# Routing by itself, then the shared MLP's eight tiles in one piece, in both mixtures of a macaron block

## The reference, cut to what matters

```
x = x + 0.5 * moe(layernorm(x))          # the first mixture
x = x + recurrence(layernorm(x))
x = x + 0.5 * moe(layernorm(x))          # the second mixture, same weights
x = x + 0.5 * ternary_mlp(layernorm(x)); x = x + linear_attention(layernorm(x)); x = x + 0.5 * ternary_mlp(layernorm(x))

moe(xf):                                  # 4096 x 128
    shared = gelu(xf @ Wfc_s + bfc_s) @ Wproj_s + bproj_s        # 128 -> 512 -> 128, all tokens
    logits = xf @ Wr                                             # 8 experts
    the two largest of each token, softmaxed over the two, are its gates
    routed = sum over the token's two experts of gate * (gelu(xf @ Wfc[e] + bfc[e]) @ Wproj[e] + bproj[e])
    return shared + routed
```

## Time and profile before

| what | value |
|---|---|
| median of 3 runs | 1436.36 us (1429.77 to 1442.43) |
| the profiled execution | 1437.86 us, of which the span of instructions is 1436.1 us |
| mean granted TensorE clock | 0.887 |
| busy | PE 1131.4 us (79%), DVE 930.1 us (65%), ACT 617.8 us (43%), POOL 606.4 us (42%) |
| chain that ended last | PE 31%, DVE 10% of the span |

### The profile page before, as it was taken

One profiled execution on the slowest core, in us unless ns is written; L12 is line 12 of the kernel. 1 busy time (PEld: TensorE's weight loads), 2 busy tenths in 40 slices (PEclk: granted clock), 3 DMA queues, 4 the chain that ended last, 5 costly groups with the idle time before them and its releaser, 6 DMA issues. The chain is left out here.

```text
span 1436.1 us, 17143 instructions
## 1 busy us (share of the span) xinstructions
PE 1131.4 (79%) x4972; PEld 813.5 (57%) x4972; DVE 930.1 (65%) x2723; ACT 617.8 (43%) x1114; POOL 606.4 (42%) x647
## 2 busy tenths in 40 slices
PE   5866999947689788878856667999944678888896
PEld 4645878835556555556635546888832444555453
DVE  6737787747767778777736437777752556565562
ACT  3325767734354454444522214777722122232322
POOL 5872000027676776665434743000036555542330
PEclk9878999988899999999976668999976699989997
DMA  7554567710000000000000105477721000000000
GB/s 232 192 205 178 162 216 234 244 68 24 10 13 12 10 10 12 12 8 1 1 0 15 48 34 174 152 241 251 227 69 34 15 14 18 20 15 8 8 15 16
DMA packets 48957, 115.42 MB, mean 80 GB/s; under 512 B 8160, under 2 KB 14304, under 8 KB 48864
## 3 DMA queue, kind: packets, MB, share of 16 engines
q1 hardware_dynamic: 40672, 97.53, 20.8%
q0 software_dynamic: 8192, 16.79, 3.9%
HBM read 79.16 MB, written 35.13 MB: 80 GB/s over the span
## 5 line engine op out<-in xcount | busy, mean ns | idle before, releaser
L642 DVE TENSOR_TENSOR hid_lo<-hid,hid_hi 128x512 fp32r<-128x512 f32 x248 | 170.3, 689 | 108.5 <-ACT hid L442 96.2
L491 POOL DMA_INDIRECT xs<-spare_all,slots x128 | 134.2, 1049 | 66.9 <-issue 37.4
L521 POOL DMA_INDIRECT got<-ys,y_slots x64 | 74.9, 1170 | 199.8 <-DMA ys<-spare_all 183.3
L521 POOL DMA_INDIRECT wr<-ys,y_slots x64 | 63.1, 985 | 193.5 <-DMA ys<-spare_all 177.0
L1068 DVE TENSOR_TENSOR_SCAN spare_all<-spare_all,carry 128x512 f32<-128x512 f32 x64 | 90.7, 1417 | 71.6 <-ACT spare_all L972 66.5
L442 ACT ACTIVATE hid<-bank,b_up_of 128x512 f32<-128x512 f32 x184 | 125.5, 682 | 6.0
L982 ACT ACTIVATE gate_b<-bank,head_rstd 128x128 f32<-128x128 f32 x256 | 72.9, 369 | 126.1 <-POOL head_rstd L1022 124.4
L219 PEld LDWEIGHTS bank<-ident,spare_all 128*128 128x128 f32 x568 | 76.3, 153 | 77.4 <-issue 68.7
L219 PE MATMUL bank<-ident,spare_all 128*128 128x128 f32 x568 | 94.6, 296 | 28.1 <-DVE spare_all L551 13.8
L441 ACT ACTIVATE hid_hi<-bank,b_up_of 128x512 fp32r<-128x512 f32 x138 | 95.1, 689 | 44.8 <-PE bank L364 34.6
L908 PE MATMUL bank<-spare_all,cw_sb 128*128 128x512 f32 x128 | 71.2, 640 | 33.3 <-DVE spare_all L1075 33.3
(11 more groups left out here) (263 smaller groups left out, 2894.0 us busy)
## 6 DMA issues: line engine op xcount, KB each, us to landing
wr<-wq SPq DMA_DIRECT2D x92, 512.0 KB, 4.6
spare_all<-xs SPq DMA_DIRECT2D x46, 256.0 KB, 4.8
ys<-spare_all SPq DMA_DIRECT2D x46, 256.0 KB, 4.9
wq<-wr SPq DMA_DIRECT2D x16, 512.0 KB
got<-in_w_mlp SPq DMA_DIRECT2D x9, 512.0 KB
xs<-X SPq DMA_DIRECT2D x16, 256.0 KB
xs<-spare_all,slots POOLq DMA_INDIRECT x128
out_x<-X SPq DMA_DIRECT2D x8, 256.0 KB, 2.3
```

Source lines behind the costliest of these rows:

```text
L491: g.indirect_dma_start(out=xs, out_offset=bass.IndirectOffsetOnAxis(ap=slots[:, k, n:n + 1], axis=0), in_=xn_all[:, n], in_offset=None).th ...
L521: nc.gpsimd.indirect_dma_start(out=rows_of(i, ring)[:, k, b], out_offset=None, in_=ys, in_offset=bass.IndirectOffsetOnAxis(ap=y_slots[:, k ...
L642: v.tensor_tensor(hid_lo[:, q], hid[:, n % HC], hid_hi[:, q].bitcast(F32), ALU.subtract).then_inc(s["lo_done"], 1)
```

## The change

`steps_beside` is gone. Each engine first runs its loop over the eight tiles with the routing alone, and then one loop over all 132 steps. In the first mixture the splits of the weights stay in the routing's loop. `find_blocks` moves from before step 16 to before step 4 of that second loop. The two waits about bank 5 go; in their place the first `back` waits that all eight tiles are copied.

```diff
@@ moe_pe
-                if backs_before_step(2 * i) > 0:
-                    pe.wait_ge(*s.at("finished", backs_before_step(2 * i)))
                 turn(pe, bank[5], lambda b: xn_all[:, i * TB + b]).then_inc(s["turned"], 1)
...
-                pe.wait_ge(*s.at("xT_ready", min(TILES, ((k + 2) * HC + 2) // 2 + 1)))
+                if k == 0:
+                    pe.wait_ge(*s.at("xT_ready", TILES))
...
-            for i in range(TILES + 1):
-                if i < TILES:
-                    find_logits(i)
-                for m, n in enumerate(steps_beside(i)):
-                    step(n)
-                    if m == 0 and i < TILES:
-                        find_places(i)
+            for i in range(TILES):
+                find_logits(i)
+                find_places(i)
                 if i + 1 < TILES:
                     turn_for_route(i + 1)
+            for n in range(STEPS + TAIL):
+                step(n)
@@ moe_act
-            for i in range(TILES + 1):
-                if first and i < TILES:
+            for i in range(TILES):
+                if first:
                     split_weights(i + 1)
-                for n in steps_beside(i):
-                    step(n)
                 if i + 1 < TILES:
                     copy_for_route(i + 1)
+            for n in range(STEPS + TAIL):
+                step(n)
@@ moe_dve
                 if first:
                     split_weights(i + 1)
-                for n in steps_beside(i):
-                    step(n)
                 find_slots(i)
             dve.wait_ge(const_ready, CONSTS)
-            find_blocks()
-            for n in steps_beside(TILES):
+            for n in range(STEPS + TAIL):
+                if n == HC:
+                    find_blocks()
                 step(n)
```

More of the change, by code:

```diff
@@ L290, in macaron_kernel @@
                     for k, n in moe_totals.items()}
[L292 to L296, removed]
         def halves(src):
```

## The result

| kernel | median of its runs | profiled execution | its span |
|---|---|---|---|
| before | 1439.22 us (1429.77 to 1442.43, 4 runs) | 1437.86 us | 1436.1 us |
| changed | 1468.32 us (1465.86 to 1473.9, 4 runs) | 1473.9 us | 1472.1 us |

The changed kernel is slower: the ratio, its time over that of the kernel before, is 1.0219 with a 95% interval of 1.0159 to 1.0279. The forecast was 1458 us, range 1414 to 1486.

A forecast was written before the change was run, and what follows sets the result against it. TensorE bounds the experts' blocks; a chain from engine to engine bounds the routing. 1437.86 - 36.5 gained + 57.6 lateness = 1459 us, put at 1458 because the profiled execution lay above the median; range 1414 to 1486.

The forecast's parts named there:

- routing R: Both mixtures' routing without steps beside it: a chain per tile, 66.4 us in the first and 62.8 in the second.
- steps T: The 32 steps of the shared blocks, run after the routing in each mixture: 54 us, with 2 us idle beside `find_blocks`.
- lateness: During POOL's unbroken scatters, TensorE's results reach their readers late: 28.8 us in each mixture, 57.6 in all.
- gain of 36.5 us: Part from first logits to block 8, without lateness: 14.8 us less in the first mixture, 21.7 in the second.
- the 20 us of the fast clock: Routing in both mixtures: if PE ran at 2.4 GHz instead of the assumed slow clock, the sum would be 20 us less.
- Share of 0.45: Part of each mixture's 64 us scatter stretch lost to late results, in routing and following steps: 28.8 us each.
- rival 3: Late results slow the routing chain to POOL's pace, so the last slots come as late as ever: 1482 us, chance 0.10.
- They end when POOL pauses: Late starts of TensorE's readers in the kernel before end when POOL's scatter stretches end, at 107.52 and 832.54 us.
- rival 2: No lateness in the changed kernel, as it needs MLP matmuls and scatters together: 1400 us, chance 0.20.
- Work of 16 steps, 26 us, thus rides on gaps: In the kernel before, 26 us of steps fill gaps of the routing chain; the change gives up that cover.
- 1: Rival: the steps absorb the lateness and only the routing suffers, 42 us in all: 1442 us, chance 0.22.
- the 3 us: POOL's scatters would shorten without the steps' DVE splits beside them, 48 in 60.4 instead of 64 us: sum 3 us lower.

The follow-up runs named there:

- undisturbed: Condition of sets 1 and 2, on two chips, without late results: the kernel before took 1389.9 and 1390.3 us.
- disturbed: Condition of the prediction's runs, its result and two later sets on one chip, with late results: there the kernel before took 1437.9 and 1430.7 us.
- set 2: Runs on one chip without late results: kernel before, unchanged, 1391.0 us; changed kernel, unchanged, 1411.21 us, ratio 1.0144; also two variants.
- the last two runs: Changed kernel unchanged, 1470.19 us; changed kernel with POOL computing two unread powers after the scatters of tiles 2 to 6, 1413.94 us; same chip.
- set 4: Runs on a chip with late results: changed kernel unchanged, 1470.19 us, ratio 1.0285; with POOL pausing on unread powers, 1413.94 us, ratio 0.9884.

## Why the prediction was right, and where not

| term | predicted | undisturbed | disturbed |
|---|---|---|---|
| routing R, first / second | 66.4 / 62.8 | 66.9 / 62.7 | 100.7 / 88.3 |
| steps T | 54 / 54 | 59.4 / 58.8 | 58.0 / 61.1 |
| lateness, both | 57.6 | 0 | 60.4 |

The number was right, and so was the size of the lateness. How the change comes to be slower was not. The forecast had a gain of 36.5 us, outweighed by lateness that the change brings. In fact the change loses 21.9 us without any lateness (spans of 1410.0 and 1388.1 us in set 2), and of the 60.4 us of lateness 48.2 were in the kernel before already: 21.9 + 60.4 - 48.2 = 34.1 of the 36.0 us. Some two thirds of the slowing are steps that lost their cover, one third is added lateness. That the result fell inside the range is in part luck: it was measured in the disturbed condition, like the base; undisturbed, the changed kernel takes 1411 us, just below the range, and is slower still than the kernel before.

**The routing**, where undisturbed, came out within half a microsecond, at the slow clock's prices: the logits take 1.87 us in both mixtures, as assumed, so the 20 us of the fast clock did not come. In the second mixture the tiles are 8.6 to 8.7 us apart with statistics and 7.6 to 7.9 without; in the first, where the splits come on top, 9.8 to 10.7 and 7.6, as worked out.

**The lateness** in the sum: 57.6 us predicted; measured, (158.65 - 126.2) + (149.42 - 121.5) = 60.4. That it is indeed lateness, and that it needs POOL's unbroken scatters beside the disturbed condition, rests on the last two runs, one chip with and without pauses. But the way in which the term was spread was wrong. "Share of 0.45", half of it in the steps, put the first step at 95 us at the latest and 850; it was at 110.35 and, less the 25.76 us by which the second mixture began later, 853.1. Of the 60.4 us, 33.8 and 25.7 lie in the two routings, under 1 in the steps. Few results are held, the worst for 13 to 18 us, and in the routing nothing can be done instead, so the chain stands and POOL runs out of slots. That is rival 3's mechanism, and in the first mixture its number, 168.3. In the second, 939.90 - 25.76 = 914.1 us lies between it (926.1) and the forecast (910.3), nearer to the forecast. The rival went wrong in what it asked for: it wanted every tile over 12 us, and two tiles of 23 and 24 us did in the first mixture, of 14 and 27 in the second, with the others at their usual length.

"They end when POOL pauses" was read too strictly. Of the five reads in the earlier trace rows, those at 90.80, 823.98 and 828.93 lie inside POOL's stretches, and so do those at 85.46 and, in the second mixture, 864.57 of the changed kernel.

**The steps** were priced too low by 5 us a mixture, and this is the 10 us between the forecast and the result. Two causes: `find_blocks` costs PE 5.5 us, not 2 (the range was 0.6 to 7), since DVE owes the steps around it the same work; in the disturbed run it was 5.14 and, behind a late gelu, 8.42. The other is what remains, 59.4 - 51.8 - 5.5 = 2.1 us, and it lies behind that idle time. The first four steps did cancel, 5.9 us (76.58 to 82.49 in the undisturbed timeline) against 6.47 for a full block. But when PE goes on at 94.17 it does so at the slow clock, granted 0.50 from 94 to 99.3: the next two steps take 5.2 us (94.17 to 99.39), where the two just ahead of the idle time take 2.9. I had no such term. Sum: 1459 + 2.8 + 10.2 = 1472, against the profiled 1473.9.

**The base** was the flaw in the argument. "Without more, 36.5 us gained" compared an undisturbed sum with a part of the kernel before that held some 48 us of lateness itself. The total didn't suffer, for the lateness was put back on the changed kernel. But rival 2's 1400 us (0.20) as a gain was never there: without late results both kernels gain, to 1390 and 1411. "Work of 16 steps, 26 us, thus rides on gaps" took the gaps as free of charge for it, and they are not. The 14 steps beside the first mixture's first seven tiles lengthen the routing by 11.9 us (72.9 - 61.0) and would, at 51.8 / 32 = 1.62 us each, cost 22.6 us behind it: a difference of 10.7, near the 11.3 us by which the part is longer.

**Rivals.** 1: right that the steps lose nothing, wrong on the size (60 us, not 42). 2: true on other chips, with another base. 3: see above. Nothing waited for weights, and block 8 had its rows in time.

**The scatter's length.** 40 scatters of the first mixture took 52.0 us against 54.8 before, 1.30 us each against 1.37. The rule cited from the Trainium skill, "GPSIMD Engine Reference", Key points, asked for a change of this sign, and the trace agrees in one thing: where DVE stands still, as from 80 to 100 us, a scatter comes every 1.26 us. But it is the holds that keep DVE still. Undisturbed, 48 scatters in a row took 65.1 us against 63.8 before in the first mixture, and 62.9 against 63.0 in the second, no shorter, and the 3 us have no part in the result.

## What to carry to other kernels

Before costing a change against a part of a trace, take out of the base what the change doesn't own: waits without a producer ("remote") are such. Here small steps that rode on a chain cost it half of what they cost behind it, so emptying the chain lost time. Where GpSimd issues many indirect transfers in a row beside chains from engine to engine, and traces show such late starts, try 2 to 3 us of other work on it every eight, and time it on more than one chip.

## What the hardware did that I had not expected

- The same kernel takes 1390 us on two chips and 1431 to 1438 on a third, with equal bytes, packets and scatters (medians 962 and 958 ns). The difference is late starts behind finished instructions, most of them TensorE's, beside indirect DMAs. What is different about the chip stays open; the traces show no more transfers on the slow one.
- All six disturbed traces hold fewer records of semaphore events, 10170 to 10578, than the eight undisturbed, 12502 to 12550, even the two with pauses, which run nearly on time. Whether the recording itself has a part in the lateness was not tested.
- Given that condition, a pause of 2.4 to 3.1 us every 8 scatters removes 56 us. But a held result need not wait for a pause: in the changed kernel of set 4 one was read at 97.35 us, 7 us before POOL's stretch ended, after 17.1 us of holding. What holds it isn't shown.
- The length of the pause and of the stretch between pauses was not varied.
